# Context taken relative to its last token, and small self-attention matmuls spread between value matmuls, in a fused attention and expert kernel

## The chip, the cores and the metric

The kernel is one program on 1 core of a Trainium2 chip. The metric is its time on the device in microseconds (us). Lower is better.

## The reference

x is 128 sequences of 32 rows of 256 features, ctx is 128 sequences of 257 tokens of 256 features. Three parts follow each other, each added to x:

```python
x = x + xattn(layernorm(x), ctx)      # 16 heads of 16, softmax over 257 tokens, no scale
x = x + attn(layernorm(x))            # rms norm, rotary positions, sigmoid weights divided by their sum, 32 x 32 a head
x = x + ffn(layernorm(x))             # 8 experts, argmax routing, 160 slots each, 256 -> 1024 (gelu) -> 256
# xattn:
k = ctx @ Wk.T + bk;  v = ctx @ Wv.T + bv
out = softmax(q @ k.T) @ v @ Wo.T + bo
```

A softmax doesn't change when one number is added to all scores of a row, and its weights sum to one. So with d(s) = ctx(s) - ctx(last), the scores may be taken with Wk d(s) + bk, and the result is the sum over the first 256 tokens of p(s) Wv d(s), plus Wv ctx(last) + bv.

## The kernel before

The rows are worked through in T = 32 tiles of 128 rows, which are four sequences. A tile's four sequences are called blocks 0 to 3 here (j in the code). Passes of a loop overlap three stages: in pass i TensorE does cross attention of tile i (xa), the output projection, norm and self-attention projections of tile i-1 (s1), and the self-attention, second norm and gate of tile i-2 (s2). After the loop, `positions` and then the expert layer run over the slots in DRAM.

A block on TensorE is: `scores` (L428) into the PSUM tile score, `keys` (L401) and `values` (L411) of the next block, `transpose_probs` (L444) of this block, and `weighted_values` (L459). Between them are the places (j, 0) to (j, 3), which the table `between` fills with short work of s1 and s2. The score tile has one buffer. VectorE takes the maxima (`maxima`, L936), ScalarE the exponentials (`exps`, L735), VectorE divides (`normalise`, L947), TensorE transposes into the same banks, VectorE and ScalarE copy out (`probsT`, L953, L764, L766), and only when `weighted_values` has had both copies can the next block's `scores` follow in TensorE's order.

Much of the short work shares one PSUM bank, shared. `turn(sem, count)` makes TensorE wait until the reader of the last user of shared is done, so that this work goes in one order.

The context has to be more exact than one pass of the fast fp32r format gives. `context_hi` (ScalarE, L751) rounds it to fp32r, `context_lo` (GpSimd, L1235) takes the rest, and keys and values are 12 matmuls each, three for each of four pairs of halves (PASSES). The last token goes its own way: `last_rows` projects all last tokens once, `last_key` (GpSimd, L1230) copies one key column into kT, `last_prob` (GpSimd, L1253) spreads its probability, `last_probs` (TensorE, L470) gathers them per tile, and `last_values` (L972) and `attended` (L965) on VectorE add the last values and b_v. Each engine runs its own list of instructions in order; `body` in each engine's section gives that order.

`self_values` (L528) is 64 small matmuls a tile, 16 heads by 4 sequences. Each works on 32 rows and 32 columns of the array and streams 17 columns; the trace holds two records for each, 128 a tile. `scores` uses 32 by 64 of the array, `scores2` (L515) and `weighted_values` 128 by 32, all else 128 by 128.

## Time and profile before

| | us |
|---|---|
| median of 3 runs (1329.96 to 1330.12) | 1329.99 |
| the profiled execution, its own time | 1326.77 |
| its span, first to last instruction | 1324.9 |
| TensorE busy (matmuls) | 1160.6 (88%) |
| VectorE busy | 851.6 (64%) |
| ScalarE busy | 801.9 (61%) |
| GpSimd busy | 568.9 (43%) |
| mean granted TensorE clock | 0.946 |

The shares are of the span. 1.9 us lie around the span in the profiled execution. Matmuls overlap, so a busy TensorE is not one at its peak.

### The profile page before, as it was taken

Reading aid. Unit: us, or ns where it says so; the run is one execution under the profiler, and the core shown is the slowest. Engines: PE = TensorE matmul, PEld = TensorE weight load, DVE = VectorE, ACT = ScalarE, POOL = GpSimd, SP = SyncE. Lnnn points to the kernel's source line nnn. Section 1 sums busy time; section 2 is a strip of 40 time slices with the busy share of each in tenths; the row PEclk is TensorE's granted clock in tenths of the full one; section 3 lists DMA queues with packets and bytes.
Section 4 is the critical chain, followed back from the end, with each engine's and each line's share of the span. In section 5 each row is a group of like instructions: output and inputs, shape, how many; then the busy total and the mean of one; then the engine's idle time right before and its main releaser. Section 6 shows DMA issues by size and latency. Waiting matters only on the chain. (4 is left out here: it accounts for less than half of the span.)

```text
span 1324.9 us, 43348 instructions
## 1 busy us (share of the span) xinstructions
PE 1160.6 (88%) x17169; PEld 980.9 (74%) x17169; DVE 851.6 (64%) x2395; ACT 801.9 (61%) x2347; POOL 568.9 (43%) x1045
## 2 busy tenths in 40 slices
PE   6898988989889889999988988998999988874897
PEld 5677777777777777777777777777787777752796
DVE  4667777776776677766677766777666667653111
ACT  5677666666666666666666766766656666632121
POOL 2344444454554444445445444444444544432021
PEclk9999999998999999989999999999888999975899
DMA  6415111111111111111111111111111111000474
GB/s 156 124 46 182 54 58 54 58 57 34 52 50 54 49 36 50 51 47 52 36 47 48 50 51 31 50 50 51 46 45 36 48 50 46 14 10 13 135 227 138
DMA packets 71927, 82.32 MB, mean 62 GB/s; under 512 B 16987, under 2 KB 50732, under 8 KB 71728
## 3 DMA queue, kind: packets, MB, share of 16 engines
q1 hardware_dynamic: 65280, 75.19, 19.3%
q0 software_dynamic: 3200, 3.71, 0.8%
q8 instruction: 138, 2.26, 0.7%
q10 hardware_dynamic: 3248, 0.66, 0.2%
q14 instruction: 61, 0.50, 0.1%
HBM read 64.79 MB, written 16.56 MB: 61 GB/s over the span
## 5 line engine op out<-in xcount | busy, mean ns | idle before, releaser
L735 ACT ACTIVATE prob<-score,nmx 128x257 f32<-128x257 f32 x512 | 236.2, 476 | 219.1 <-DVE nmx L936 218.8
L401 PE MATMUL kps<-ctx_p,wk_p 128*128 128x256 f32 x1536 | 217.4, 292 | 0.3 <-POOL ctx_p L1235 0.2
L411 PE MATMUL vps<-wv_p,ctx_p 128*128 128x256 f32 x1536 | 214.7, 289 | 0.0
L401 PEld LDWEIGHTS kps<-ctx_p,wk_p 128*128 128x128 f32 x1536 | 200.0, 196 | 6.1 <-issue 1.9
L1235 POOL TENSOR_TENSOR ctx_p<-ctxT,ctx_p 128x512 fp32r<-128x512 f32 x128 | 152.3, 1190 | 117.1 <-ACT ctx_p L751 116.7
L411 PEld LDWEIGHTS vps<-wv_p,ctx_p 128*128 128x128 f32 x1536 | 191.5, 191 | 12.4 <-issue 12.4
L936 DVE TENSOR_REDUCE nmx<-score 128x2 f32<-128x514 f32 x256 | 165.2, 687 | 51.7 <-PE score L428 51.7
L1253 POOL TENSOR_TENSOR plast<-const,prob 128x128 f32<-128x128 f32 x128 | 64.1, 501 | 255.8 <-DVE prob L947 255.8
L947 DVE TENSOR_SCALAR prob<-prob,rsum 128x257 f32<-128x257 f32 x512 | 158.5, 352 | 9.0
L953 DVE COPY probT<-score 128x512 f32<-128x512 f32 x96 | 66.4, 691 | 126.2 <-PE score L444 125.9
L444 PE MATMUL score<-const,prob 128*128 128x128 f32 x1024 | 140.8, 281 | 2.3 <-DVE prob L947 2.1
L444 PEld LDWEIGHTS score<-const,prob 128*128 128x128 f32 x1024 | 119.1, 144 | 11.4 <-DVE prob L947 4.0
L744 ACT ACTIVATE kT<-kps,b_k 128x256 f32<-128x256 f32 x256 | 110.2, 497 | 23.9 <-PE kps L401 22.6
L459 PE MATMUL gather<-probT,vv 128*32 128x64 f32 x4096 | 99.7, 235 | 21.3 <-DVE probT L953 18.0
L766 ACT ACTIVATE probT<-score 128x512 f32<-128x512 f32 x128 | 76.5, 598 | 62.8 <-PE score L444 62.5
L459 PEld LDWEIGHTS gather<-probT,vv 128*32 128x32 f32 x4096 | 77.7, 116 | 48.0 <-issue 39.8
L735 ACT ACTIVATION_READ_ACCUMULATOR prob<-score,nmx 128x1 f32 x512 | 105.0, 205 | 0.0
L428 PE MATMUL score<-kT,qz 32*64 32x257 f32 x2048 | 94.7, 427 | 1.3 <-issue 1.3
L757 ACT ACTIVATE vv<-vps 128x512 f32<-128x512 f32 x128 | 78.0, 610 | 17.4 <-PE vps L411 17.4
L1270 POOL TENSOR_TENSOR qks<-qk,const 128x256 f32<-128x256 f32 x32 | 43.6, 1362 | 100.6 <-DVE qk L1003 100.6
L751 ACT ACTIVATE ctx_p<-ctxT 128x512 fp32r<-128x512 f32 x128 | 82.7, 646 | 0.3 <-DMA ctxT<-in_ctxT 0.3
L528 PE MATMUL shared<-v2a,th 32*32 32x17 f32 x4096 | 53.9, 183 | 30.4 <-issue 27.9
(159 smaller groups left out, 2029.3 us busy)
## 6 DMA issues: line engine op xcount, KB each, us to landing
ctxT<-in_ctxT SPq DMA_DIRECT2D x128, 257.0 KB, 3.0
w<-in_w SPq DMA_DIRECT2D x16, 1024.0 KB, 8.7
xq<-in_x SPq DMA_DIRECT2D x32, 128.0 KB, 3.2
xr<-in_x SPq DMA_DIRECT2D x32, 128.0 KB, 2.1
qbd<-qkT SPq DMA_DIRECT2D x256, 16.0 KB, 1.9
out<-row SPq DMA_DIRECT2D x32, 128.0 KB, 1.9
slots<-row SPq DMA_DIRECT2D x10, 257.0 KB, 5.6
x_a<-slots SPq DMA_DIRECT2D x8, 129.0 KB, 2.1
```

Source lines behind the costliest of these rows:

```text
L401: last = mm(kps[:, c, :], wk_p[:, x, n, c * P:(c + 1) * P], ctx_p[:, g, y, n, :], start=(n, x) == (0, LO), stop=(n, y) == (C - 1, LO))
L411: last = mm(vps[:, c, :], ctx_p[:, g, x, n, c * P:(c + 1) * P], wv_p[:, y, n, :], start=(n, x) == (0, LO), stop=(n, y) == (C - 1, LO))
L428: last = mm(score[64 * e:64 * e + 64, m, 0:S], qz[rows, half, e, j, :, :].rearrange("p h q -> p (h q)"), kT[rows, b_slot(j), e, :], start= ...
L444: last = nc.tensor.transpose(score[:, 2 * c, at:at + P], prob[:, 2 * c + g, n * P:(n + 1) * P], k["ident"])
L459: last = mm(gather[32 * g:32 * g + 32, c, :, j * L:(j + 1) * L], vv[:, b_slot(j), n, c * P + 32 * g:c * P + 32 * g + 32], probT[:, c, n, 2 ...
L735: last = af(prob[:, m, :], score[:, m, 0:S], ACT.Exp, bias=nmx[:, m:m + 1], scale=1.0, accum_out=esum[:, m:m + 1])
L744: last = af(kT[:, j % 2, c, 0:SM], kps[:, c, :], ACT.Identity, bias=b_k[:, c:c + 1], scale=1.0)
L751: af(ctx_p[:, g, HI, :, :], ctxT[:, r, :, g, 0:SM], ACT.Copy).then_inc(s["ctx_hi"], 1)
L757: af(vv[:, j % 2], vps[:, :, :], ACT.Copy).then_inc(s["v_evac"], 1)
L936: v.tensor_reduce(nmx[:, 2 * c:2 * c + 2], score[:, 2 * c:2 * c + 2, 0:S], AX.X, ALU.max, negate=True).then_inc(s["max_done"], 1)
L947: last = v.tensor_scalar(prob[:, m, :], prob[:, m, :], rsum[:, m:m + 1], None, ALU.mult)
L1235: g.tensor_tensor(ctx_p[:, g_, LO, :, :], ctxT[:, r, :, g_, 0:SM], ctx_p[:, g_, HI, :, :].bitcast(F32), ALU.subtract).then_inc(s["ctx_part ...
```

## The change

Keys and values are computed from the context minus its last token. ScalarE's `context_hi` subtracts it while it rounds (two instructions of 256 columns with a bias, in place of one of 512), and `context_lo` goes from GpSimd to VectorE (two instructions with two inputs and a per-partition scalar). The last key is then b_k for every block, written once, and the last value enters `extract` as vlast, which holds b_v too. `last_key`, `last_prob`, `last_probs`, `attended` and the per-tile `last_values` fall away. `even_heads` of att goes from ScalarE into `extract` on VectorE. The parts of y1 go from GpSimd to ScalarE (`rows_hi`) and VectorE (`rows_lo`), without the copy y1T.

In TensorE's order, 12 of the 16 heads of `self_values` go between the 12 value matmuls of block 1, one head of 4 small matmuls behind each; the other 4 heads follow at (1, 3). `scores2` moves from (0, 1) to (0, 0), `positions` to (0, 2), the transposes of y1 to (1, 2), `transpose_qk` from block 2 to (3, 0), `project_queries` from (1, 0) to (3, 1), the transposes of y2 to (3, 2) and `gate` to (3, 3). `choose` and `gate_exp` move into block 0 of the next pass. SyncE loads xq ahead of the second half of the context.

```diff
-    def values(t, j):
+    def values(t, j, aside=None):
         b, g = TB * t + j, j % 2
         pe.wait_ge(s["v_evac"], b)
+        if aside is not None:
+            self_ready(aside)
         for c in range(C):
             for n in range(C):
-                for x, y in PASSES:
+                for at, (x, y) in enumerate(PASSES):
                     last = mm(vps[:, c, :], ctx_p[:, g, x, n, c * P:(c + 1) * P], wv_p[:, y, n, :],
                               start=(n, x) == (0, LO), stop=(n, y) == (C - 1, LO))
-        last.then_inc(s["v_done"], 1)
+                    if (n, at) == (C - 1, len(PASSES) - 1) and c == C - 1:
+                        last.then_inc(s["v_done"], 1)
+                    if aside is not None:
+                        self_head((c * C + n) * len(PASSES) + at)
...
-    def self_values(t):
+    def self_ready(t):
+        turn("att2n_done", t + 1)
         pe.wait_ge(s["sig_flat"], t + 1)
         pe.wait_ge(s["v2_done"], t + 1)
         if once(t):
             pe.wait_ge(s["zeroed"], 2)
...
+    def self_head(h):
+        for j in range(TB):
+            rows = slice(32 * j, 32 * j + 32)
+            last = mm(shared[rows, h * (HD + 1):(h + 1) * (HD + 1)], th[rows, h * L:(h + 1) * L], v2a[rows, h, :],
+                      start=True, stop=True)
+        if h == H - 1:
+            last.then_inc(s["pv2_ps"], 1)
+    def self_values(t, beside):
+        if not beside:
+            self_ready(t)
+        for h in range(C * C * len(PASSES) if beside else 0, H):
+            self_head(h)
...
         between = {
-            (0, 0): s1 and (lambda: (turn("att_tmp", t1 + 1), last_probs(t1))),
-            (0, 1): lambda: (t3 is not None and positions(t3),
-                             s2 and (turn("relu_done", t2 + 1), scores2(t2))),
-            (0, 2): s1 and (lambda: (turn("x1_step", 3 * t1 + 1), project_out(att, wo, "att_done", t1, "o1_ps"))),
+            (0, 0): s2 and (lambda: (turn("relu_done", t2 + 1), scores2(t2))),
+            (0, 2): lambda: (t3 is not None and positions(t3),
+                             s1 and (turn("x1_step", 3 * t1 + 1),
+                                     project_out(att, wo, "ext_step", 2 * t1 + 2, t1, "o1_ps")),
+                             once(i) and (turn("vlast_done", C), last_rows())),
             (0, 3): q and (lambda: (turn("xnT_done", i + 2), transpose_queries(i + 1))),
-            (1, 0): q and (lambda: (turn("qT_done", i + 2), project_queries(i + 1))),
-            (1, 1): s1 and (lambda: (spare_free(xa, i, 1), transpose_rows(y1, "y1_done", t1, "y1t_ps", spare_c))),
-            (1, 2): s2 and (lambda: (turn("att2n_done", t2 + 1), self_values(t2))),
+            (1, 2): s1 and (lambda: (spare_free(xa, i, 1), transpose_rows(y1, "y1_done", t1, "y1t_ps", spare_c))),
+            (1, 3): s2 and (lambda: self_values(t2, xa)),
             (2, 0): s1 and (lambda: (turn("qk_done", t1 + 1), project_qk(t1))),
             (2, 1): s2 and (lambda: (spare_free(xa, i, 2), transpose_rows(att2n, "att2n_done", t2, "at2_ps", spare_c))),
-            (2, 2): s2 and (lambda: (turn("x2_step", 3 * t2 + 1), project_out(att2, ao, "att2_done", t2, "o2_ps"))),
-            (2, 3): s1 and (lambda: (turn("qkT_done", t1 + 1), transpose_qk(t1))),
-            (3, 0): s2 and (lambda: (turn("y2T_done", t2 + 1), transpose_rows(row, "y2_done", t2, "y2t_ps", sh_c))),
-            (3, 1): s2 and (lambda: (turn("logit_done", t2 + 1), gate(t2))),
-            (3, 3): s1 and (lambda: (spare_free(xa, i, 3), project_v2(t1))),
+            (2, 2): s2 and (lambda: (turn("x2_step", 3 * t2 + 1), project_out(att2, ao, "att2_done", t2 + 1, t2, "o2_ps"))),
+            (3, 0): s1 and (lambda: (turn("qkT_done", t1 + 1), transpose_qk(t1))),
+            (3, 1): q and (lambda: (turn("qT_done", i + 2), project_queries(i + 1))),
+            (3, 2): s2 and (lambda: (turn("y2T_done", t2 + 1), transpose_rows(row, "y2_done", t2, "y2t_ps", sh_c))),
+            (3, 3): lambda: (s2 and (turn("logit_done", t2 + 1), gate(t2)),
+                             s1 and (spare_free(xa, i, 3), project_v2(t1))),
         }
...
             if ahead:
-                values(ta, ja)
+                values(ta, ja, t2 if j == 1 and s2 else None)
...
     def context_hi(t, j):
         b, r, g = TB * t + j, j // 2, j % 2
         act.wait_ge(ctx_in[r], 16 * C * (t + 1))
         act.wait_ge(s["v_done"], floor0(b - 1))
-        af(ctx_p[:, g, HI, :, :], ctxT[:, r, :, g, 0:SM], ACT.Copy).then_inc(s["ctx_hi"], 1)
+        for c in range(C):
+            last = af(ctx_p[:, g, HI, c, :], ctxT[:, r, c, g, 0:SM], ACT.Identity, bias=nlast[:, c, b:b + 1], scale=1.0)
+        last.then_inc(s["ctx_hi"], 1)
...
+    def rows_hi(t):
+        act.wait_ge(s["y1t_ps"], t + 1)
+        act.wait_ge(s["v2_ps"], t)
+        af(y1T_p[:, HI], spare_c, ACT.Copy).then_inc(s["y1T_hi"], 1)
...
-            if j == 0 and s1:
-                act.wait_ge(s["o1_ps"], t1)
-                even_heads(att, gather[:, :, 0, :], "pv_done", TB * (t1 + 1), "ext_step")
...
+            if xa and (j < 2 or q):
+                context_hi(*((i, j + 2) if j < 2 else (i + 1, j - 2)))
+            if j == 0 and i >= 3:
+                gate_exp(t2 - 1)
+            if j == 3 and s1:
+                act.wait_ge(s["qbd2_in"], 16 * HH * t1)
+                copy_rows(qkT[:, :, :].rearrange("p c n -> p (c n)"), shared[:, :], "qkt_ps", t1, "qkT_done")
             if xa:
                 exps(i, j)
-            if j == 1 and q:
-                queries(i + 1, 1 - half)
-            if j == 1 and s1:
-                copy_rows(y1T[:, :, :], spare_c, "y1t_ps", t1, "y1T_done")
             if ahead:
                 keys(ta, ja)
             if j == 0 and s2:
...
                 copy_rows(att2[:, :, :], spare_c, "at2_ps", t2, "att2_done")
             if j == 1 and s1:
                 squares(t1)
-            if j == 3 and s2:
-                gate_exp(t2)
+            if j == 3 and q:
+                queries(i + 1, 1 - half)
             if ahead:
                 values(ta, ja)
-            if xa and j < 3 and (j < 2 or q):
-                context_hi(*((i, j + 2) if j < 2 else (i + 1, j - 2)))
+            if j == 1 and s1:
+                rows_hi(t1)
+            if j == 3 and s2:
+                copy_rows(y2T[:, :, :], sh_c, "y2t_ps", t2, "y2T_done")
             if j == 0 and s2:
                 sigmoid_abs(t2)
             if xa:
                 probsT(i, j)
             if j == 0 and s2:
                 sigmoid_exp(t2)
-            if xa and j == 3 and q:
-                context_hi(i + 1, 1)
             if j == 0 and q:
                 copy_rows(xnT[:, :, :], sh_c, "qt_ps", i + 1, "xnT_done")
-            if j == 2 and s1:
-                act.wait_ge(s["qbd2_in"], 16 * HH * t1)
-                copy_rows(qkT[:, :, :].rearrange("p c n -> p (c n)"), shared[:, :], "qkt_ps", t1, "qkT_done")
     tiles(body)
+    gate_exp(T - 1)
...
+    def context_lo(t, j):
+        b, r, g = TB * t + j, j // 2, j % 2
+        dve.wait_ge(s["ctx_hi"], b + 1)
+        for c in range(C):
+            last = v.scalar_tensor_tensor(ctx_p[:, g, LO, c, :], ctxT[:, r, c, g, 0:SM], nlast[:, c, b:b + 1],
+                                          ctx_p[:, g, HI, c, :].bitcast(F32), ALU.add, ALU.subtract)
+        last.then_inc(s["ctx_parts"], 1)
...
-                last = v.tensor_scalar(prob[:, m, :], prob[:, m, :], rsum[:, m:m + 1], None, ALU.mult)
+                last = v.tensor_scalar(prob[:, m, 0:SM], prob[:, m, 0:SM], rsum[:, m:m + 1], None, ALU.mult)
...
     def extract(t):
+        dve.wait_ge(s["pv_done"], TB * (t + 1))
+        dve.wait_ge(s["o1_ps"], t)
+        if once(t):
+            dve.wait_ge(s["vlast_done"], C)
+        v.scalar_tensor_tensor(att[:, :, :].rearrange("p c (j q) -> p c j q", j=TB),
+                               gather[:, :, 0, :].rearrange("p c (j q) -> p c j q", j=TB), k["even"],
+                               vlast[:, t, :, :].unsqueeze(3).to_broadcast([P, C, TB, L]), ALU.mult, ALU.add
+                               ).then_inc(s["ext_step"], 1)
         dve.wait_ge(s["ext_step"], 2 * t + 1)
         v.scalar_tensor_tensor(att[:, :, :], gather[:, :, 1, :], k["odd"], att[:, :, :], ALU.mult, ALU.add
                                ).then_inc(s["ext_step"], 1)
...
+    def last_values():
+        dve.wait_ge(s["last_ps"], 1)
+        for c in range(C):
+            v.tensor_scalar(vlast[:, :, c, :], sh_c[:, c].rearrange("p (t j) -> p t j", j=TB), b_v[:, c:c + 1], None,
+                            ALU.add).then_inc(s["vlast_done"], 1)
...
+    def rows_lo(t):
+        dve.wait_ge(s["y1T_hi"], t + 1)
+        v.tensor_tensor(y1T_p[:, LO], spare_c, y1T_p[:, HI].bitcast(F32), ALU.subtract).then_inc(s["y1T_parts"], 1)
...
+        if xa:
+            maxima(i, 0)
+            context_lo(i, 2)
+        if i >= 3:
+            choose(t2 - 1)
+        if s1:
+            extract(t1)
+        if once(i):
+            norm_x(1)
+        if xa:
+            normalise(i, 0)
+        if q:
+            norm_x_apply(i + 1)
+        if i >= 3:
+            position(t2 - 1)
+        if s1:
+            residual1(t1)
+        if xa:
+            probsT(i, 0)
+        if s1:
+            residual1_stats(t1)
+            residual1_mean(t1)
+        if once(i):
+            last_values()
+        if s2:
+            sigmoid_product(t2)
+        if s1:
+            norm1(t1)
+        if xa:
+            maxima(i, 1)
+            context_lo(i, 3)
+        if xa:
+            normalise(i, 1)
+        if xa:
+            probsT(i, 1)
+        if s1:
+            rows_lo(t1)
+        if s2:
+            inverse2(t2)
+            weigh2(t2)
+        if xa:
+            maxima(i, 2)
+        if s1:
+            evac_qk(t1)
+        if xa:
+            normalise(i, 2)
+        if s1:
+            rope_products(t1)
+        if q:
+            context_lo(i + 1, 0)
+        if s1:
+            rope_add(t1)
+        if s2:
+            residual2(t2)
+            residual2_stats(t2)
+            residual2_mean(t2)
+        if once(i):
+            setup_scales()
+        if xa:
+            maxima(i, 3)
+        if s2:
+            norm2(t2)
+        if q:
+            context_lo(i + 1, 1)
+        if xa:
+            normalise(i, 3)
+            probsT(i, 3)
+        if norms_ahead(i):
+            norm_x(i + 2)
+        if s2:
+            logits(t2)
+        if s1:
+            evac_v2(t1)
...
+    choose(T - 1)
...
+        if once(i):
+            power("q", "xn_stat", 6, 1, "xn_pow")
+        if s1:
+            residual_bias(t1)
+            power("1", "x1_done", t1 + 1, t1, "x1_pow")
+        if i >= 3:
+            slot_numbers(t2 - 1)
+            send(t2 - 1)
+        if s1:
+            rms(t1)
+        if s1:
+            rope_sin(t1)
+        if s2:
+            power("2", "x2_done", t2 + 1, t2, "x2_pow")
+        if norms_ahead(i):
+            power("q", "xn_stat", 3 * (i + 3), i + 2, "xn_pow")
+        if s1:
+            residual_bias2(t1)
```

## Rows read from the trace of the kernel before

**Rows 1.** The page: span, and the busy time of each engine.
```profile
span 1324.9 us, 43348 instructions
...
PE 1160.6 (88%) x17169; PEld 980.9 (74%) x17169; DVE 851.6 (64%) x2395; ACT 801.9 (61%) x2347; POOL 568.9 (43%) x1045
```

**Rows 2.** Windows view; us, busy of each engine, granted clock, DMA share, GB/s.
```profile
420.00:425.00 5.00, 4.52 (x134) 3.16 (x135) 1.52 (x5) 1.54 (x3) 3.80 (x9) 0.68 0.13 34
```

**Rows 3.** Source view of L716, once per tile, from 400 to 1120 us.
```profile
L716 ACT ACTIVATE att<-gather,const x20: 475/475/475, 402.9 to 1101.7; 128x256 f32<-128x256 f32 x20
```

**Rows 4.** Timeline, TensorE, one tile: the scores that open each block (start, us).
```profile
878.63 0.69 PE L428 MATMUL score<-kT,qz 32*64 32x257 f32 x16
...
889.48 0.69 PE L428 MATMUL score<-kT,qz 32*64 32x257 f32 x16
...
899.07 0.69 PE L428 MATMUL score<-kT,qz 32*64 32x257 f32 x16
...
907.52 0.69 PE L428 MATMUL score<-kT,qz 32*64 32x257 f32 x16
...
914.39 0.69 PE L428 MATMUL score<-kT,qz 32*64 32x257 f32 x16
```

**Rows 5.** Timeline, TensorE, block 0 of the same tile.
```profile
879.25 1.16 PE L470 MATMUL shared<-plast,const 128*128 128x128 f32 x8
...
883.49 1.07 PE L515 MATMUL shared<-qbd,qkT 128*32 128x256 f32 x16 [1.09 <-DVE alast L972]
```

**Rows 6.** Timeline, TensorE, block 1 of the same tile.
```profile
892.66 1.68 PE L411 MATMUL vps<-wv_p,ctx_p 128*128 128x256 f32 x12
...
894.42 0.56 PE L528 MATMUL shared<-v2a,th 32*32 32x17 f32 x45
...
896.10 0.88 PE L528 MATMUL shared<-v2a,th 32*32 32x17 f32 x77 [0.50 <-issue]
```

**Rows 7.** Timeline, TensorE, narrow windows at two changes of matmul shape.
```profile
883.95 0.61 PE L515 MATMUL shared<-qbd,qkT 128*32 128x256 f32 x8
884.49 0.50 PE L411 MATMUL vps<-wv_p,ctx_p 128*128 128x256 f32 x2
...
896.68 0.30 PE L528 MATMUL shared<-v2a,th 32*32 32x17 f32 x14
896.91 0.33 PE L444 MATMUL score<-const,prob 128*128 128x128 f32 x1
```

**Rows 8.** Source views of L411 and L528: ns min/median/max of one matmul.
```profile
L411 PE MATMUL vps<-wv_p,ctx_p x1536: 278/283/387, 16.6 to 1164.7; 128*128 128x256 f32 x192
...
L528 PE MATMUL shared<-v2a,th x4096: 172/178/232, 95.5 to 1210.9; 32*32 32x17 f32 x196
```

**Rows 9.** VectorE: source view of L1075, then timeline rows of blocks 0.
```profile
L1075 DVE TENSOR_SCALAR pr<-ex,rse x32: 231/1162/1172, 114.1 to 1221.5; 128x8 f32<-128x8 f32 x32
...
916.21 0.23 DVE L1085 TENSOR_SCALAR oh<-eqr,top 128x8 bf16<-128x8 f32 x1
...
885.58 0.71 DVE L965 SCALAR_TENSOR_TENSOR att<-alast,b_v,att 128x128 f32<-128x128 f32 x2
```

**Rows 10.** Timeline, VectorE and ScalarE, the softmax of block 3; VectorE copy of block 0.
```profile
888.01 0.69 DVE L953 COPY probT<-score 128x512 f32<-128x512 f32 x1
...
908.29 1.29 DVE L936 TENSOR_REDUCE nmx<-score 128x2 f32<-128x514 f32 x2
...
909.20 0.47 ACT L735 ACTIVATE prob<-score,nmx 128x257 f32<-128x257 f32 x1
...
911.00 0.86 ACT L744 ACTIVATE kT<-kps,b_k 128x256 f32<-128x256 f32 x2
...
911.36 0.62 DVE L947 TENSOR_SCALAR prob<-prob,rsum 128x257 f32<-128x257 f32 x2
```

**Rows 11.** Timeline, ScalarE block 1, and SyncE queue block 3.
```profile
892.85 1.52 ACT L724 ACTIVATE qz<-shared,b_qz,const 128x128 f32<-128x128 f32 x4
...
907.70 5.04 SPq L257 DMA_DIRECT2D qbd<-qkT  x8
```

224 lines of the change are left out of this document (39 added, 185 removed).

## The prediction

> **What bounds the kernel now.** I read the page first: TensorE is busy for 88% of the span, VectorE 64%, ScalarE 61%, GpSimd 43% [rows 1]. An average says little about what sets the order, so I went to one tile in the middle. A once-per-tile instruction starts 20 times between 402.9 and 1101.7 us [rows 3], which is 698.8 / 19 = 36.78 us a tile. The scores of one undisturbed tile start at 878.63, 889.48, 899.07 and 907.52, the next tile's at 914.39 [rows 4], so its blocks take 10.85, 9.59, 8.45 and 6.87, together 35.76. The missing 1.02 us a tile is clock: in a window of another tile just behind the self-attention matmuls, the granted clock is 0.68 [rows 2], so part of it ran at 1.2 instead of 2.4 GHz.
>
> TensorE does the work in order and its list is nearly full, but within a block there is also a ring: the score bank has one buffer. In block 3, scores start at 907.52, VectorE's maxima run 908.29 to 909.58, the exponentials 909.20 to 911.00, the last division ends at 911.98 [rows 10]. So transposes can't finish before about 4.9 us into a block, plus whatever VectorE or ScalarE has queued in between. Copies and weighted values follow (0.7 each [rows 10], the latter an estimate by the copy). A block is therefore about 6.3 us at least, and everything inserted on VectorE between these steps counts once TensorE has no work to cover it. The visible waits of TensorE in this tile are 1.09 for `last_values` in block 0 [rows 5] and gaps between small matmuls in block 1 [rows 6].
>
> **The change, block by block.** I lay out a pass anew, with time 0 at the block's scores. Estimates are of my making from the rows named.
>
> The new prices. `context_lo` on VectorE is two instructions of 256 columns with a scalar and two inputs. The nearest row is two of 128 columns in 0.71 [rows 9]; 128 columns more each, at the 1.29/2/514 us a column of the maxima [rows 10], give 0.71 + 2 x 0.16 = 1.03. The division pair of 0.62 [rows 10] is the lower end. I take 1.0, four times a tile. `extract` is now two such instructions, one after the other: 1.0 too. `choose` has seven tiny steps; its row L1075 has median 1.16 and minimum 0.23 [rows 9], and it took the long time where GpSimd's `context_lo` ran. With that gone I take 0.23, and 7 x 0.2 = 1.4 for the whole. On ScalarE, `context_hi` becomes two pieces, 0.86 by the two key copies [rows 10] in front of the exponentials, where ScalarE is free at a block's start: nothing is paid while the exponentials wait for the maxima at 1.5 anyway.
>
> Block 0. VectorE: maxima to 2.05, `context_lo` to 3.05, `choose` to 4.45, `extract` to 5.45, both divisions 1.55 to 7.0. TensorE: scores, `scores2`, keys, values end near 4.65 (0.6 + 1.0 + 1.5 + 1.5; 1.5 for twelve large matmuls at the spacing worked out below). Then it waits: `positions` needs `choose` and `extract`, the projection needs `extract`. At 5.55 it goes on, the second half of the transposes waits for 7.1, ends 7.5. VectorE still has xn, position and residual1 (1.2 by estimate: three short ones of 0.4, a third of the 1.29 for 514 columns each) ahead of its copy, which ends at 7.05 + 1.2 + 0.69 = 8.95. Weighted values end at 9.65. So block 0 falls from 10.85 to 9.65: `last_probs` (0.9 of its 1.16, which overlaps what follows [rows 5]) and the wait of 1.09 [rows 5] go, a wait of 0.9 behind `choose` and `extract` comes.
>
> Block 1 is where the change decides. A large value matmul lasts 0.283, a small one 0.178 [rows 8]; twelve large in 1.68 [rows 6] start every (1.68 - 0.283) / 11 = 0.127. When the shape changes, no overlap is left but 0.07: the `scores2` matmuls end at 884.56 and the first large one starts at 884.49; the small ones end at 896.98 and the next starts at 896.91 [rows 7]. And the first large one behind a change takes 0.387 [rows 8]: in rows 7 two of them take 0.50, so the second starts 0.50 - 0.283 = 0.217 behind the first instead of 0.127. The small records run at (0.88 - 0.178) / 76 = 0.0092 [rows 6]. One large matmul and a head of 8 records then cost 0.387 - 0.07 (to the first small one) + 7 x 0.0092 + 0.178 - 0.07 (to the next large one) = 0.49. If the large one isn't slowed, it is 0.39; if changes cost nothing, 0.127 + 8 x 0.0092 = 0.20. I take 0.49, since the 0.387 belongs to this very instruction. Twelve steps are 5.9 us, and the four heads at (1, 3), with a change on each side, 0.21 + 31 x 0.0092 + 0.11 = 0.6. Before, the values start at 892.66 and the transposes at 896.91 [rows 6, 7]: 4.25 for both. Now 6.5. The gaps between small ones, about 0.9 of the 4.25 [rows 6], are won and are already in this.
>
> The page "TensorEngine Tiling (Array Packing)" of the Trainium skill, section Key Properties, says the same of a change of tiling mode, that it drains TensorE; it gives no price. The page "TensorE: Matmul & The Clock Gate", section Measured speedup and its mechanism, lets weight loads be pulled ahead of matmuls in flight when row groups don't conflict. By that rule the large one would not be slowed and the step would be 0.39, 1.2 us a tile less; the 0.387 of rows 8 speaks against it.
>
> The rest of block 1: scores and keys 2.1 (`project_queries` has left), values with heads to 8.0, transposes of y1 and of the probabilities to 8.95, heads to 9.55; ScalarE copies values, y1 and the second half in turn after 8.0, 0.6 to 0.7 each and 0.4 for y1, until 9.7; weighted values end at 10.1. VectorE's late maxima (1.85, behind `norm1`) and `context_lo` are covered by the long stretch. 9.59 becomes 10.1.
>
> Block 2: `transpose_qk` leaves; the copies on ScalarE set the end as before. I take 8.2 for 8.45. `rows_lo` and the division of the self-attention end 0.5 into it, just free for the maxima. `context_lo` sits behind the divisions; with the rotary work and residual2 it makes VectorE 0.3 late for block 3.
>
> Block 3 gets `transpose_qk` (0.6), `project_queries` (0.9 as `last_probs`) and all of s2's y2 and gate: scores, qkT, keys, queries, values reach 5.1. Then the y2 transposes use the shared bank behind ScalarE's `queries`. ScalarE: exponentials to 3.75, keys 0.86 [rows 10], `queries` 1.52 [rows 11], so 6.15. TensorE waits 1.15, and what it holds up are the probability transposes and all behind: transposes 7.15, gate and v2 8.45, weighted 9.1. 6.87 becomes 9.1. The diagonal DMAs on SyncE are eight issues in 5.04 us [rows 11]; ScalarE's copy ends at 1.9, they are issued by 7.0 and, with some 2 us to land by my estimate, are in by 9, before `scores2` at 9.7. That cover is 0.7 us; xq and the context loads ahead of them are issued much earlier.
>
> **Sum.** 9.65 + 10.1 + 8.2 + 9.1 = 37.05 against 35.76. The clock: the stretch with small matmuls gets longer, not shorter, so I keep the loss of 1.02, 38.07 against 36.78, +1.29. It applies to the 30 tiles with all stages: +38.7. The start loses `last_rows` ahead of the first scores and the first tiles get lighter: -4 by estimate. The experts stay. The profiled execution took 1326.77, its span 1324.9; the median shown is 1329.99, 3.2 more. 1326.8 + 34.7 = 1361.5 in the profile's measure, and with 3.2 more 1364.7; I say **1364**.
>
> **Rivals.** (1) Changes of shape cost nothing in the middle of a stream, or the heads hide behind the large matmuls. A step is 0.20, block 1 is bound by the softmax ring and ScalarE at about 8.1. 35.05 + 1.02 = 36.07, -0.71 a tile, -25: 1305. This is the faster side. It decides below 0.38 a step, since there the sum meets 35.76. For it: the gaps in rows 6 show that small ones alone don't flow. Against: both changes in rows 7. Chance 0.20.
> (2) The waits I put in blocks 0 and 3 (0.9 and 1.15) are hidden, by a ScalarE or VectorE that is earlier than I lay out. -2.05 a tile: 1303. Against: both orders are strict. Chance 0.12.
> (3) Spreading keeps the clock at 2.4 GHz: 37.05 against 36.78, +8 - 4: 1334. Chance 0.10.
> (4) The long stretch of draining steps falls to 1.2 GHz in every tile, a second 1.0 to 1.3 us: 1364 + 36 = 1400. For it: the 0.68 of rows 2 stands right behind the small matmuls. Chance 0.10.
> Forecast: 0.48.
>
> **Numbers.** Slower are the forecast, (4) and most of (3): 0.64. Faster are (1) and (2) with a little off, 0.29. 0.2% is 2.7 us, about what a measurement of this kernel can tell from no change: 0.07. The bounds: 0.39 a step gives 1364 - 36 = 1328, `context_lo` at 0.62 instead of 1.0 takes up to 0.4 off block 0, 12 in all. With the rivals the range is 1292 to 1400. The forecast's own is 1335 to 1385.
>
> **What would show it.** Right: in block 1 the value matmuls take about 6 us with small ones between, each step near 0.49; block 3 near 9 with TensorE waiting for ScalarE's qz ahead of the y2 transposes; block 0 under 10 with a wait behind att. Wrong: steps of 0.2 to 0.3, or blocks 0 and 3 shorter by a microsecond each.

## The result and the profile after

The changed kernel takes 1389.2 us (1384.46 to 1392.94, four runs), the kernel before 1329.97 (1326.40 to 1330.12, four runs). The ratio is 1.045, with a 95% interval of 1.041 to 1.049: slower by 59 us, where 1364 was forecast with a range of 1292 to 1400. The profiled execution of the changed kernel took 1384.46, its span 1382.4, so like for like it is 57.7 us above that of before.

The page of the changed kernel, span and busy time; against [rows 1] TensorE is busier by 93 us, GpSimd has lost half its work, VectorE has gained 46 us:

```profile
span 1382.4 us, 42435 instructions
...
PE 1254.0 (91%) x16905; PEld 1023.2 (74%) x16905; DVE 897.3 (65%) x2622; ACT 827.1 (60%) x2441; POOL 296.5 (21%) x597
```

The source view of the first instruction of `extract`, once per tile, which stands where [rows 3] stood:

```profile
L965 DVE SCALAR_TENSOR_TENSOR att<-gather,const,vlast x19: 478/478/480, 429.5 to 1127.5; 128x256 f32<-128x256 f32 x19
```

19 of them lie 698.0 us apart from first to last. A tile takes 698.0 / 18 = 38.78 us against 36.78, +2.00. Both views leave tiles out. By the starts of all scores, the 29 tiles in which all three stages run and another tile follows take 38.69 on average against 36.39: +2.30 a tile, 66.6 us in all. What lies before them is 3.7 us shorter than before, what lies behind them (the last tile and the experts) 5.4 us. So more than the whole loss is in the full tiles.

The timeline of TensorE over one tile, the counterpart of [rows 4, 6, 7]: the scores that open blocks 3, 0, 1, 2 and 3, the first steps of block 1 and one at its end, and transposes of the probabilities:

```profile
880.47 0.69 PE L425 MATMUL score<-kT,qz 32*64 32x257 f32 x16
...
886.44 0.44 PE L471 MATMUL shared<-const,row 128*128 128x128 f32 x2 [0.94 <-ACT qz L722]
...
889.64 0.69 PE L425 MATMUL score<-kT,qz 32*64 32x257 f32 x16
...
898.41 0.69 PE L425 MATMUL score<-kT,qz 32*64 32x257 f32 x16
...
900.57 0.28 PE L404 MATMUL vps<-wv_p,ctx_p 128*128 128x256 f32 x1
900.77 0.25 PE L519 MATMUL shared<-v2a,th 32*32 32x17 f32 x8
900.96 0.38 PE L404 MATMUL vps<-wv_p,ctx_p 128*128 128x256 f32 x1
901.27 0.25 PE L519 MATMUL shared<-v2a,th 32*32 32x17 f32 x8
901.45 0.38 PE L404 MATMUL vps<-wv_p,ctx_p 128*128 128x256 f32 x1
...
905.90 0.58 PE L404 MATMUL vps<-wv_p,ctx_p 128*128 128x256 f32 x1
...
907.13 1.91 PE L441 MATMUL score<-const,prob 128*128 128x128 f32 x8
...
910.56 1.16 PE L425 MATMUL score<-kT,qz 32*64 32x257 f32 x16
...
917.56 1.04 PE L441 MATMUL score<-const,prob 128*128 128x128 f32 x8
...
919.72 0.69 PE L425 MATMUL score<-kT,qz 32*64 32x257 f32 x16
```

Blocks 3, 0, 1 and 2 take 9.17, 8.77, 12.15 and 9.16. Inside block 1 a value matmul starts 0.49 or 0.50 us after the one before (900.96, 901.45) in 258 of the 319 steps of the 29 full tiles. The first step of each tile takes 0.39 (900.57 to 900.96): there the large matmul has no small ones in front of it and lasts 0.28 instead of 0.38. 24 steps take 0.75, at the low clock shown below, and the other eight lie between. At 905.90 the same matmul lasts 0.58 instead of 0.38, and the eight transposes of the probabilities take 1.91, where those of block 2 take 1.04. The windows view cuts this tile there (us, busy time of each engine, granted clock, DMA share, GB/s):

```profile
898.40:904.50 6.10, 6.10 (x106) 4.45 (x101) 4.50 (x13) 3.94 (x15) 3.87 (x11) 1.00 0.34 97
904.50:910.50 6.00, 6.00 (x110) 4.79 (x110) 1.79 (x5) 2.37 (x5) 1.50 (x3) 0.62 0.06 19
```

In the first six microseconds of block 1 the granted clock is full, in the next six it is 0.62, so much of that stretch runs at 1.2 instead of 2.4 GHz. This happens in all 29 full tiles: in none is block 1 shorter than 11.4 us, and in each the granted clock falls in block 1.

VectorE in block 0 of the same tile, the counterpart of [rows 9]:

```profile
891.60 0.87 DVE L932 SCALAR_TENSOR_TENSOR ctx_p<-ctxT,nlast,ctx_p 128x256 fp32r<-128x256 f32 x2
...
892.58 0.23 DVE L1083 TENSOR_SCALAR pr<-ex,rse 128x8 f32<-128x8 f32 x1
...
893.64 0.48 DVE L965 SCALAR_TENSOR_TENSOR att<-gather,const,vlast 128x256 f32<-128x256 f32 x1
894.15 0.48 DVE L970 SCALAR_TENSOR_TENSOR att<-gather,const,att 128x256 f32<-128x256 f32 x1
```

`context_lo` takes 0.87 for its pair, the small division of `choose` 0.23 in all 32 tiles (median 1.16 before), `extract` 0.48 twice.

### The profile page after: what moved, and what is told of

Its sections match the earlier page's. It is cut to its first block, busy times and chain, and to the rows that moved or that the text cites. A ratio compares the mean times of both kernels' runs of the same rounds, so it can differ in the third digit from the quotient of the medians.

```text
span 1382.4 us, 42435 instructions
## 1 busy us (share of the span) xinstructions
PE 1254.0 (91%) x16905; PEld 1023.2 (74%) x16905; DVE 897.3 (65%) x2622; ACT 827.1 (60%) x2441; POOL 296.5 (21%) x597
## 4 chain that ended last, share of the span: by engine, by line
PE 63%; DVE 16%; ACT 12%; issue 5%; DMA 2%; SPq 2%; POOL 0%; POOLq 0%; DVEq 0%; ACTq 0%
PE vps L404 12%; PE kps L392 7%; PE gather L456 7%; PE shared L519 6%; PE score L441 6%; PE score L425 6%; PE shared L480 4%; ACT prob L732 4%; ACT qz L722 3%; DVE nmx L940 3%; PE score L678 2%; DVE prob L951 2%; PE score L664 2%; PE shared L465 2%; ACT kT L741 2%
## 5 line engine op out<-in xcount | busy, mean ns | idle before, releaser
L404 PE MATMUL vps<-wv_p,ctx_p 128*128 128x256 f32 x1536 | 305.6, 313 | 0.0
L404 PEld LDWEIGHTS vps<-wv_p,ctx_p 128*128 128x128 f32 x1536 | 219.3, 193 | 9.7
L951 DVE TENSOR_SCALAR prob<-prob,rsum 128x256 f32<-128x256 f32 x512 | 177.4, 389 | 9.1
L441 PE MATMUL score<-const,prob 128*128 128x128 f32 x1024 | 160.8, 308 | 4.6 <-DVE prob L951 4.3
L441 PEld LDWEIGHTS score<-const,prob 128*128 128x128 f32 x1024 | 141.6, 161 | 12.9 <-DVE prob L951 6.7
L1263 POOL TENSOR_TENSOR rstd<-ve,const 128x1 f32<-128x1 f32 x64 | 48.0, 749 | 413.6 <-DVE ve L994 259.1
L519 PEld LDWEIGHTS shared<-v2a,th 32*32 32x32 f32 x4096 | 76.6, 120 | 64.4 <-issue 24.7
L519 PE MATMUL shared<-v2a,th 32*32 32x17 f32 x4096 | 116.2, 199 | 3.5 <-issue 3.5
L750 ACT ACTIVATE ctx_p<-ctxT,nlast 128x256 fp32r<-128x256 f32 x256 | 115.5, 504 | 0.6 <-issue 0.6
L932 DVE SCALAR_TENSOR_TENSOR ctx_p<-ctxT,nlast,ctx_p 128x256 fp32r<-128x256 f32 x256 | 111.6, 477 | 5.9 <-ACT ctx_p L750 5.9
```

Source lines behind the costliest of these rows:

```text
L404: last = mm(vps[:, c, :], ctx_p[:, g, x, n, c * P:(c + 1) * P], wv_p[:, y, n, :], start=(n, x) == (0, LO), stop=(n, y) == (C - 1, LO))
L441: last = nc.tensor.transpose(score[:, 2 * c, at:at + P], prob[:, 2 * c + g, n * P:(n + 1) * P], k["ident"])
L519: last = mm(shared[rows, h * (HD + 1):(h + 1) * (HD + 1)], th[rows, h * L:(h + 1) * L], v2a[rows, h, :], start=True, stop=True)
L750: last = af(ctx_p[:, g, HI, c, :], ctxT[:, r, c, g, 0:SM], ACT.Identity, bias=nlast[:, c, b:b + 1], scale=1.0)
L932: last = v.scalar_tensor_tensor(ctx_p[:, g, LO, c, :], ctxT[:, r, c, g, 0:SM], nlast[:, c, b:b + 1], ctx_p[:, g, HI, c, :].bitcast(F32), A ...
L951: last = v.tensor_scalar(prob[:, m, 0:SM], prob[:, m, 0:SM], rsum[:, m:m + 1], None, ALU.mult)
```

## The experiments

Twelve kernels ran, on four chips. Each is compared with runs of the kernel before on its own chip, and there the kernel before took 1279 to 1281 us, not 1330. Why is the first thing to settle; the other comparisons hold by their ratios.

To compare blocks, I took the starts of the scores from each trace and averaged each block over the 29 full tiles, the third to the 31st. In us, worked out from these starts:

```
kernel                        ratio (95%)              block 0  1      2     3     tile
before, again                 1.000 (0.998 to 1.002)   10.79   8.86   8.45  6.86  34.96
changed, again                1.090 (1.087 to 1.093)    8.79  12.25   8.68  9.21  38.93
e6: groups of two             0.991 (0.988 to 0.993)    8.78   8.50   8.24  9.21  34.73
e10: six single, six at once  1.009 (1.006 to 1.012)    8.79   9.34   8.23  9.19  35.54
e2: groups of four            0.971 (0.968 to 0.973)    8.79   7.61   8.28  9.19  33.87
e1: all sixteen together      0.981 (0.977 to 0.985)    8.79   7.76   8.50  9.19  34.24
e8: full-shape in between     1.005 (1.004 to 1.007)    8.79   8.82   8.24  9.19  35.03
e4: y2 later                  1.067 (1.064 to 1.071)    8.79  12.31   8.39  8.46  37.94
e5: groups of four + y2 later 0.954 (0.952 to 0.956)    8.79   7.64   8.31  8.45  33.19
e12: e5 + work on GpSimd      0.958 (0.955 to 0.961)    8.78   7.67   8.32  8.57  33.33
e3: before + single heads     1.214 (1.211 to 1.217)   10.83  16.87   9.31  6.86  43.87
e7: before + groups of four   1.058 (1.056 to 1.061)   10.83  11.35   8.51  6.86  37.55
```

The profiles of the result, worked out the same way, have 10.74, 9.85, 8.99, 6.81 before (36.39) and 8.83, 12.10, 8.56, 9.19 after (38.69). Below, the low clock in a tile means that the granted clock falls in its block 1 or 2.

**The two controls.** No edit. For the kernel before:

> The kernel before, unaltered, profiled here, since it took 1280 us beside all eleven runs so far and 1330 in the result, with the changed kernel at 1390 in both. Theory A (the difference is low clock): the blocks' usual lengths are those of the profile before (10.85, 9.6, 8.45, 6.87), and fewer of them are lengthened; the tile is 35.2 instead of 36.4 us. Theory B (the gaps of 0.50 us between the small matmuls of block 1 are gone here): block 1 is 8.6 to 8.8 us in nearly every tile and the rest as it was.

It took 1279.1 us against 1278.8 for the other copy. TensorE in block 1 of one of its tiles, then two windows of it:

```profile
892.49 0.69 PE L428 MATMUL score<-kT,qz 32*64 32x257 f32 x16
...
895.67 1.67 PE L411 MATMUL vps<-wv_p,ctx_p 128*128 128x256 f32 x12
897.42 1.75 PE L528 MATMUL shared<-v2a,th 32*32 32x17 f32 x128
...
901.26 0.69 PE L428 MATMUL score<-kT,qz 32*64 32x257 f32 x16
```

```profile
400.00:700.00 300.00, 275.23 (x4517) 232.82 (x4515) 220.90 (x620) 207.63 (x609) 151.61 (x281) 1.00 0.17 49
```

The 128 small matmuls stand in one row of 1.75 us, where [rows 6] has gaps of 0.36 and 0.50 in them. The gaps have shrunk rather than gone. Record by record, the small matmuls stop behind the 45th and the 51st in 23 of the 29 tiles of the profile before, with about 0.55 and 0.68 from start to start; here they stop behind the 45th (0.15) and the 64th or 65th (0.27) in 23 of 29. From the first start to the last it is 2.39 us there and 1.57 here (medians); with no stop it is 1.08 (e1, below). Block 1 takes 8.77 instead of 9.59, and in 27 of 29 tiles no more than 9.3. The granted clock is 1.00, where the same window of the profile before has 0.96; the low clock comes in 15 of the 29 tiles there and in none here. So both theories were half right: of the 1.43 us between the tiles, 36.39 and 34.96, block 1 holds 0.99 and block 2, which follows it, 0.54. 0.82 of it is the gaps (9.59 - 8.77), most of the rest the low clock. The gaps sit at the same records in most tiles of a profile, so they seem tied to a place in the program, which no run tests; what sets their length stayed open. The kernel before was profiled on this one of the four chips alone, on the others only its time says that it was as fast.

For the changed kernel:

> The changed kernel itself, unaltered, as the control of this chip, on which the kernel before took 1280 us in the first four runs where it took 1330 in the result. If the loss of the change is in TensorE's steps and in a low clock that comes with them in every tile, it doesn't shrink with the kernel before: near 1390 us, a ratio of 1.08 or 1.09 to the kernel before. If the chip's clock lowers or lifts both alike: 1.045, 1340 us.

It took 1394.6 us, a ratio of 1.090, as first expected. The changed kernel is as slow in both places; only what it is compared with moves. The tiles differ by 38.93 - 34.96 = 3.97, times 29 = 115 us, and the medians by 115.5.

**The heads together again.** The last matmuls of the sixteen heads behind the y1 transposes, the rest as changed:

```diff
-                        values(ta, ja, t2 if j == 1 and s2 else None)
+                        values(ta, ja)
...
-                    (1, 3): s2 and (lambda: self_values(t2, xa)),
+                    (1, 2): lambda: (s1 and (... transpose_rows(y1, "y1_done", t1, "y1t_ps", spare_c)),
+                                     s2 and self_values(t2, False)),
```

> The changed kernel with the sixteen heads of the self-attention together again, behind the value matmuls of block 1 (and behind the y1 transposes), all else as changed. Theory (the step of one value matmul and one head costs 0.495 us against 0.14 + 0.16 = 0.30 when they stand apart, and the low clock of block 1 follows from it): block 1 falls from 11.7 to 12.8 us to about 8.5, so 3.5 us a tile or about 100 us in all: near 1290 us (1275 to 1310), with the granted clock back at 0.95 or more. Rival A (the change of shape costs only what the steps show, and the low clock has another cause): block 1 falls by 2.3 us alone, about 1320 us, with the clock still at 0.92 to 0.93. Rival B (the loss sits in other edits): within 10 us of 1389.

1255.6 us, 0.981 of the kernel before and so about 139 us under the changed kernel (0.109 x 1279). That is more than expected, because the heads in one run cost less than I had put (TensorE, block 1):

```profile
908.46 0.69 PE L425 MATMUL score<-kT,qz 32*64 32x257 f32 x16
...
910.61 1.60 PE L404 MATMUL vps<-wv_p,ctx_p 128*128 128x256 f32 x12
...
912.36 1.26 PE L519 MATMUL shared<-v2a,th 32*32 32x17 f32 x128
...
915.71 0.69 PE L425 MATMUL score<-kT,qz 32*64 32x257 f32 x16
```

128 small records start within 1.26 - 0.178 = 1.08 us, 0.0085 each. Block 1 is 7.25, and its end is then set by the softmax ring (TensorE waits 0.44 for VectorE's copy ahead of the weighted values), not by the matmuls. It is the interleaving that makes the change slow; everything else in it together is a gain of 1.9%, and no run separates the parts of that gain. In 9 of its 29 tiles block 1 is longer, 8.0 to 10.2: each has one gap of TensorE, 0.4 to 1.8 us, in which it waits for nothing that the profile shows. Two of the nine gaps lie among the small matmuls, and three of the nine tiles have the low clock as well.

**Fewer places.** The edit puts four heads behind every fourth value matmul, two behind every second, and one behind each of the first six with six behind the last:

```diff
-                            if aside is not None:
-                                self_head((c * C + n) * len(PASSES) + at)
+                            step = (c * C + n) * len(PASSES) + at
+                            if aside is not None and step % 4 == 3:      # e6: step % 2 == 1
+                                for h in range(step - 3, step + 1):      # e6: range(step - 1, ...)
+                                    self_head(h)
```

> The changed kernel with four heads behind every fourth value matmul (three places) where it has one head behind each of twelve; the last four heads stay where they are. Theory (a price for each change between the large and the small shape, 0.20 us a pair): nine pairs fewer, 1.8 us a tile, plus what the clock gives back, 0 to 1.5 us: between 1345 and 1295 us, and a quarter of the way back from the run with the heads together. Rival (the price hangs on the small matmuls being beside large ones at all, not on the number of changes): less than 10 us gained.

0.971, 1241.9 us, better than the theory's best case and than the run with the heads together: the clock came back whole, not by a part (granted clock 1.00 from 600 to 900 us, where the two profiles of the changed kernel have 0.94 and 0.91; the low clock in none of the 29 tiles). TensorE, one group:

```profile
869.71 0.74 PE L404 MATMUL vps<-wv_p,ctx_p 128*128 128x256 f32 x4
870.38 0.44 PE L521 MATMUL shared<-v2a,th 32*32 32x17 f32 x32
870.75 0.74 PE L404 MATMUL vps<-wv_p,ctx_p 128*128 128x256 f32 x4
```

Four and four take 1.04 us. Against 4 x 0.495 that saves 0.94 for three pairs of changes: 0.313 a pair.

> The changed kernel with two heads behind every second value matmul: six places. A step of one value matmul and one head takes 0.495 us and one of four and four 1.04 us, so (4 x 0.495 - 1.04) / 3 = 0.31 us for a pair of changes of shape, and two and two should take 0.495 x 2 - 0.31 = 0.68 us. Theory (linear in the number of changes): the stretch takes 6 x 0.68 = 4.1 us against 5.94 with twelve places and 3.12 with three: 1.0 us a tile above the run with groups of four while the clock holds, 0.995 of the kernel before; if the low clock comes in every tile here too, up to 1.04. Rival (the clock follows the number of changes with a jump, not the price): the step is under 0.6 us.

0.991. A narrow window of TensorE:

```profile
888.54 0.51 PE L404 MATMUL vps<-wv_p,ctx_p 128*128 128x256 f32 x2
888.98 0.31 PE L521 MATMUL shared<-v2a,th 32*32 32x17 f32 x16
889.22 0.50 PE L404 MATMUL vps<-wv_p,ctx_p 128*128 128x256 f32 x2
```

A step of two and two takes 0.675 or 0.68, as forecast. The three steps fit 0.315 us for a pair of changes and 0.18 for each value matmul with its head: 0.495, 0.675, 1.035. (This is a fit. Against the pieces taken alone, 0.127 [rows 6, 8] and 8 x 0.0085, a step of one and one costs 0.30 more, one of four and four 0.26.) The rival is out as far as the price goes, but it has a point on the clock: block 1 is 8.5 in 28 of 29 tiles and the low clock comes in none, while with twelve places no tile kept the full clock.

> The changed kernel with one head behind each of the first six value matmuls, and the next six heads together behind the twelfth: seven places. Theory A (the price is the number of changes, and the low clock needs a long stretch of single steps): the stretch takes 6 x 0.495 + 6 x 0.127 + 0.6 = 4.3 us, block 1 8.8 us, no low clock: 1.00 of the kernel before. Theory B (single steps by themselves bring the low clock, however few): 1.5 to 2.3 us a tile more, 1.035 to 1.055.

1.009, between the theories and nearer A. Block 1 takes 8.8 or 8.9 in 19 of 29 tiles and 10.2 or 10.3 in ten. The windows view of one of the ten, and a row of TensorE in it:

```profile
692.00:698.00 6.00, 6.00 (x146) 5.13 (x146) 2.24 (x9) 2.98 (x9) 2.38 (x5) 0.72 0.32 94
```

```profile
692.82 1.36 PE L404 MATMUL vps<-wv_p,ctx_p 128*128 128x256 f32 x6
```

Six value matmuls in 1.36, right behind the sixth single step; at the spacing of 0.127 they would take about 0.9 to 1.0. Six single steps bring the low clock in a third of the tiles, twelve in all, six double steps in none (e6), three groups of four in none (e2; in e5, in one of 29). So it isn't the number of changes alone: the same six changes, spaced by twice the work, keep the clock. What else decides it (e10's ten tiles show no rhythm that I could name) stays open.

**Is it the shape?** Each head's four small matmuls are replaced by one of the full shape; the product with the values is left out, so the output isn't the reference's:

```diff
-                for j in range(TB):
-                    rows = slice(32 * j, 32 * j + 32)
-                    last = mm(shared[rows, ...], th[rows, h * L:(h + 1) * L], v2a[rows, h, :], ...)
+                last = mm(shared[:, h * (HD + 1):(h + 1) * (HD + 1)], k["ident"], v2a[:, h, :], ...)
```

> The changed kernel with one matmul of the full shape (128 x 128 weights, the unit matrix, 17 columns) in place of each head's four small ones; the product of the self-attention with its values is left out and its output is v2 itself. The twelve places stay. Theory (it is the change of shape that drains TensorE): without it a step takes 0.13 us for the value matmul and 0.10 to 0.15 for the other, about 0.26, block 1 is as short as with the heads together (7.3 to 7.6), the clock is back at 0.96 or more: 0.97 to 0.985 of the kernel before. Rival (putting any other matmul between two of one accumulation costs the same): the step stays at 0.4 us or above and the time at 1.03 or above.

1.005, between the two. A narrow window of TensorE in block 1:

```profile
895.78 0.37 PE L404 MATMUL vps<-wv_p,ctx_p 128*128 128x256 f32 x1
895.99 0.29 PE L517 MATMUL shared<-v2a,const 128*128 128x17 f32 x2
896.12 0.36 PE L404 MATMUL vps<-wv_p,ctx_p 128*128 128x256 f32 x1
```

A step takes 0.345. The last four heads of this kernel, eight such records in a row, start within 0.90, 0.112 each, so two of them and one value matmul cost 2 x 0.112 + 0.127 = 0.35 when nothing alternates. Interleaving one shape with itself is free; my 0.10 to 0.15 for the other matmul was too low, and that is the miss. With the change of shape, a step costs 0.495 for a head that alone takes 0.07 (8 x 0.0085). So the loss belongs to the change of shape (e8 also has one matmul where the head has four; but the price falls with the number of changes in e6 and e2, where the small matmuls are the same). The clock goes with it: block 1 is 8.81 to 8.83 in all 29 tiles, with twelve single alternations and no low clock in any.

The duration of the large matmul needs care. It is 0.36 or 0.37 here too, with no change of shape anywhere near, so it doesn't mark a drain by itself. But here the next matmul starts 0.21 after it (895.78, 895.99), well inside its duration, while in the changed kernel the head starts 0.31 after a large matmul of 0.38 (900.96, 901.27), only 0.07 before its end. With a change of shape the longer duration counts in full, without one it is overlapped.

The Trainium skill, page "TensorEngine Tiling (Array Packing)", section Key Properties, has the rule that changing the tiling mode drains TensorE; these runs agree with it (0.07 us of overlap at a change, 0.16 without one), and put 0.315 us on a pair of changes.

**The interleaving alone, in the kernel before.** The same edit of `values`, `self_head` and `self_values`, nothing else:

> The kernel before with one edit of the change alone: one head behind each value matmul of block 1, the last four behind them. Theory: block 1 gets 12 steps of 0.495 us for 4.25 - 0.6 us of separate work, so 2.3 us more, and 1 to 1.5 us of low clock more: 3.3 to 3.8 us a tile, about 1330 + 105 = 1435 us (1395 to 1450). Rival (the loss comes from the context's low parts, the queries' slot or the routing, and the interleaving is nearly free): under 1345 us.

1.214, 1552 us, far beyond the theory. Block 1 grew by 8.0, from 8.86 to 16.87. A wait of 1.59 is in front of the first value matmul. TensorE's timeline there and at the end of the stretch, then ScalarE's row at the time of the wait:

```profile
886.35 0.35 PE L413 MATMUL vps<-wv_p,ctx_p 128*128 128x256 f32 x1 [1.59 <-issue]
...
892.58 0.58 PE L413 MATMUL vps<-wv_p,ctx_p 128*128 128x256 f32 x1
...
893.75 1.97 PE L449 MATMUL score<-const,prob 128*128 128x128 f32 x8
```

```profile
884.74 1.52 ACT L740 ACTIVATE qz<-shared,b_qz,const 128x128 f32<-128x128 f32 x4
```

The heads write the shared bank, which the queries of the next tile still hold until ScalarE has copied them out (884.74 + 1.52 = 886.26). Before, the wait for them lay behind the value matmuls, which covered it; interleaved, it lies ahead of the value matmuls, and all twelve are queued behind it. Then a few steps of 0.49 come, then steps of 0.75 at the low clock (228 of the 319 in the 29 tiles), and the transposes (1.97) and weighted values (1.30) run at the low clock too. In the change the queries have moved to block 3, so this wait isn't there; here two of its edits depend on each other.

> The kernel before with the heads in three groups of four between the value matmuls of block 1, and no other edit. There one head behind each value matmul took block 1 from 9.85 to 16.85 us, of which 1.6 is a wait ahead of the values for the queries' evacuation, which held the shared bank. Theory (the wait stays, the changes of shape fall from twelve to three, the low clock goes): block 1 near 10.9 us, about 1.02 of the kernel before. Rival A (groups are a gain wherever they stand): 1.00 or less. Rival B (the low clock comes with the wait): 1.05 or more.

1.058. The wait is there (1.55), and without disturbance block 1 is 10.5 to 11.0, as the theory has it; but 10 of 29 tiles take 12.4 to 13.0, and these are the ones with the low clock. Rival B was right on the time, and the low clock came with groups of four, which kept it in e2. A stretch of changes behind a pause of TensorE fares worse than one without; that is a comparison of two kernels that differ in more than the pause, so it is a hint and no proof.

**The wait for the queries.** The y2 transposes behind those of the probabilities, the gate behind v2:

```diff
-                    (3, 2): s2 and (lambda: (turn("y2T_done", t2 + 1), transpose_rows(row, ...))),
-                    (3, 3): lambda: (s2 and (turn("logit_done", t2 + 1), gate(t2)),
-                                     s1 and (spare_free(xa, i, 3), project_v2(t1))),
+                    (3, 3): lambda: (s2 and (turn("y2T_done", t2 + 1), transpose_rows(row, ...)),
+                                     s1 and (spare_free(xa, i, 3), project_v2(t1)),
+                                     s2 and (turn("logit_done", t2 + 1), gate(t2))),
```

> The changed kernel with the transposes of y2 in block 3 moved from in front of the transposes of the probabilities to behind them, and the gate behind the v2 projection, so that nothing on TensorE waits for the queries' evacuation. Theory (the 0.95 to 1.15 us wait for the queries stands on the path): block 3 falls from 9.17 to about 8.2, 0.95 us x 30 = 28 us: near 1361 us. Rival (ScalarE's order then holds the transposed probabilities back, whose evacuation stands behind the same queries): the wait reappears in front of the weighted values, and the time stays within 8 us of 1389.

1.067 against 1.090, 29 us less. Block 3 of the undisturbed tiles falls by 0.73, from 9.18 to 8.45, and not by the whole wait of 0.94: the next limit is v2, whose evacuation the scores of the following block wait for by 0.26. The low clock of block 1 stayed (12.31 against 12.25).

> The changed kernel with both mends: heads in three groups of four between the value matmuls, and the y2 transposes behind those of the probabilities. Theory (the two waits are in different blocks and add): block 3 falls from 9.17 to 8.45 as it did with the second mend alone, 0.72 us a tile, 21 us in all: from 0.970 of the kernel before to 0.954, about 1221 us where before takes 1280. Rival (with block 1 short again, another ring, that of the diagonal DMAs or of v2, takes the gain back): 0.965 or more.

0.954, 1220.3 us, as forecast, and the fastest version here. TensorE, the end of block 3; the transposes of y2 follow those of the probabilities without a wait, and the new limit is the 0.26 of the last row:

```profile
905.14 1.04 PE L443 MATMUL score<-const,prob 128*128 128x128 f32 x8
906.24 0.44 PE L473 MATMUL shared<-const,row 128*128 128x128 f32 x2
...
907.24 0.58 PE L536 MATMUL shared<-gw,y2T 128*128 128x8 f32 x4
...
908.70 0.69 PE L427 MATMUL score<-kT,qz 32*64 32x257 f32 x16 [0.26 <-DVE v2a L1028]
```

**GpSimd beside VectorE.** e5, and on GpSimd four times a tile:

```diff
+                pool.wait_ge(s["ctx_hi"], b + 1)
+                pool.wait_ge(s["idle_done"], b - 1)
+                g.tensor_tensor(idle_b[:, :], idle_a[:, :], idle_a[:, :], ALU.subtract).then_inc(s["idle_done"], 1)
```

> The version with both mends (0.954 of the kernel before), and on GpSimd, in the four places where the kernel before had the context's low parts, one more subtraction of 512 columns on a buffer of its own, whose result nobody reads. Theory (GpSimd's large subtractions made VectorE's tiny steps long: 1.16 against 0.23 us for one of 8 columns): the steps of choose in block 0 grow by about 0.9 us, the wait ahead of the projection with them, 0.9 x 30 = 27 us: 0.975. Rival (VectorE's steps are long for another reason, or block 0 has room): within 0.002 of 0.954.

0.958, near the rival. The added subtraction of block 0 ran ahead of the maxima and was over 2 us ahead of the small division of `choose`, which stayed at 0.23 in all tiles: the experiment missed its aim. What it does show is block 2. The first row is VectorE with the added work, the next two GpSimd at the same time, the last VectorE in e5:

```profile
865.71 2.02 DVE L954 TENSOR_SCALAR prob<-prob,rsum 128x256 f32<-128x256 f32 x2
```

```profile
865.68 0.85 POOL L1288 TENSOR_TENSOR qks<-qk,const 128x256 f32<-128x256 f32 x1 [1.85 <-DVE qk L1012]
866.50 1.09 POOL L1267 TENSOR_TENSOR idle_b<-idle_a 128x512 f32<-128x512 f32 x1
```

```profile
861.44 1.24 DVE L953 TENSOR_SCALAR prob<-prob,rsum 128x256 f32<-128x256 f32 x2
```

The pair of divisions, 0.62 undisturbed, takes 1.24 beside one GpSimd instruction and 2.02 beside two. It cost little, since block 2's end is set by ScalarE's copies; the 0.14 a tile that was lost is mostly in block 3 (8.57 against 8.45). The page "SBUF — State Buffer" of the Trainium skill, section Who interferes with whom, has VectorE and GpSimd share a pair of ports, of which the one that issues first holds the other off for its whole instruction, and names tensor_scalar, as these divisions are, among the instructions that can take it; these rows agree.

For the 1.16 of `choose` the profile of the kernel before has the evidence that e12 missed. Its small division took 1.16 or 1.17 in 24 of 32 tiles, and in each of these GpSimd's `context_lo` had started 0.04 or 0.05 us ahead of it and ended 0.02 or 0.03 ahead of it. In the eight tiles where the division took 0.23, `context_lo` started later or not beside it at all. One tile of each kind:

```profile
878.54 1.19 POOL L1235 TENSOR_TENSOR ctx_p<-ctxT,ctx_p 128x512 fp32r<-128x512 f32 x1 [1.83 <-ACT ctx_p L751]
878.59 1.16 DVE L1075 TENSOR_SCALAR pr<-ex,rse 128x8 f32<-128x8 f32 x1
...
331.15 0.23 DVE L1075 TENSOR_SCALAR pr<-ex,rse 128x8 f32<-128x8 f32 x1
331.21 1.22 POOL L1235 TENSOR_TENSOR ctx_p<-ctxT,ctx_p 128x512 fp32r<-128x512 f32 x1 [1.78 <-ACT ctx_p L751]
```

## Why the prediction was right, and which term was off

**The step of a value matmul and a head: right, to the hundredth.** 0.49 was forecast, 0.495 measured, in every step at full clock but the first. Both terms stand in the rows: the large matmul lasts 0.38 and overlaps the head by 0.07 (0.31 from start to start), and 0.185 later the next large one starts. The price is a change of shape, as said (e8); the 0.387 alone doesn't prove one, since the large matmul is as long in e8, but at a change it counts in full. By the rule on weight loads that the prediction takes from the Trainium skill (on the page "TensorE: Matmul & The Clock Gate" it stands in the section The mechanism), the step would have been 0.39. It was, only where no head stood in front of the large matmul.

**Block 1 without the clock: 10.1 forecast, 10.4 inferred.** No tile of the changed kernel shows it undisturbed. From e6, whose tiles are: 8.49 + 12 x 0.495 - 6 x 0.675 = 10.38.

**The clock: this term was mis-sized.** I kept the loss of before, 1.02 us a tile. Measured is 12.10 - 10.38 = 1.72 in block 1, and 8.56 - 8.23 = 0.33 in block 2 into which the low stretch reaches: 2.05. That is rival 4, with a chance of 0.10: the stretch falls to 1.2 GHz in every tile. Its 1.0 us more a tile is just what came. The reason I gave the forecast the higher chance was that the clock loss of before would carry over as it is; the control shows that this loss belonged to those runs (the kernel before has the low clock in no full tile in its other profile), while the changed kernel has it in every full tile of both its profiles. Nor was it 1.02 on average: that was 36.78 from 19 tiles less one undisturbed tile, and over all 29 it was 36.39 - 35.76 = 0.63. Rival 3 (the clock stays up) was the opposite of what came.

**Block 0: 9.65 forecast, 8.78 measured.** It hid most of the miss in the clock. `context_lo` is 0.87 and not 1.0, `choose` takes 1.25 and not 1.4, `extract` 1.0 as forecast, so `att` is ready at 4.99 and not 5.45; the wait of TensorE for `att` is 0.50 (9.7 us in 19 tiles) and not 0.9. And the three short operations that I laid in front of VectorE's copy of the probabilities, 1.2 us, run while TensorE does the projection and the transposes; the copy starts at 7.33 into the block and I had 8.25.

**Block 2: 8.2 forecast, 8.23 measured. Block 3: 9.1 forecast, 9.17 measured**, with a wait for the queries of 0.94 on the matmul itself and 1.14 on its weight load in nearly every tile, where I had 1.15. Rival 2 is out for block 3; e4 shows what it would have been worth, 0.73 a tile and not 1.15, since v2 is next in line.

**The sum, and what was luck in it.** Undisturbed, the blocks give 8.78 + 10.38 + 8.23 + 9.17 = 36.56, and with the low clock (2.05, and 0.07 in blocks 0 and 3) the measured 38.69, against 38.07: about +1.1 of clock and +0.3 of block 1, -0.87 of block 0. But the loss is counted from the kernel before, whose tile was 36.39 and not 36.78. So the 29 full tiles lost 66.6 us where 38.7 was forecast. The start gave back 3.7, as forecast (4). The last tile and the experts gave back 5.4, which the prediction had at nothing. 66.6 - 3.7 - 5.4 = 57.5 against 34.7: that is the 23 us between 1361.5, the forecast in the profile's measure, and 1384.5. The mechanism of the step was foreseen; that the time came near the forecast, and not at rival 4's 1400, is luck in part, since block 0 and the end of the kernel, both wrongly sized, hid much of the error in the clock.

**The faster side.** Rival 1 said that if changes of shape cost nothing, the kernel would be faster by 25 us. They do cost; but take them out (e1) and the same change is 1.9% faster than before, with three groups of four 2.9%, with the later y2 4.6%. So the gain in block 0, 10.79 to 8.79, where `last_probs` fell away and the routing wait became smaller (their shares were not separated), was real; more than that was spent in block 1, 3.4 us, and in block 3, 2.3 us (which partly is only work moved there).

## What to carry to other kernels

Small tiled matmuls that are to run in the gaps of large ones must come in groups: here each pair of changes of shape cost about 0.3 us, one head of work 0.07, and four heads at a time were better than one, two and sixteen. Price an interleaving by the spacing of the starts at a change that the trace already has, and count the changes; then ask what the added stretch does to the granted clock, because that came on top here, 2.0 us of low clock for 3.1 us of longer steps (10.38 against 7.27 with the heads together). When an instruction moves ahead of others in a queue, its waits move with it: e3 lost 1.6 us a tile to a wait that had been free.
